# One fp32 matmul an image in place of three fp32r passes, with the identity added by VectorE

## The reference

```python
q, k, v = Wq x, Wk x, Wv x              # per image, 8 heads of 16 channels
k = softmax(k, axis=-2)                 # over the 16 channels of a head
context = einsum('bhdn,bhen->bhde', k, v)
out = einsum('bhdn,bhde->bhen', q, context)
y = einsum('oc,bchw->bohw', Wo, out) + x
mean, var = mean(y, axis=(0, 2, 3)), var(y, axis=(0, 2, 3))
result = (y - mean) * rsqrt(var + 1e-5) * gamma + beta
```

## Time and profile before

| | us |
|---|---|
| median of 3 runs | 53.73 |
| the runs | 52.9, 53.73, 54.81 |
| span of the profiled execution | 51.0 |
| TensorE busy | 37.5 |
| VectorE busy | 34.3 |
| ScalarE busy | 27.2 |
| GpSimd busy | 18.6 |

### The profile page before, as it was taken

One profiled execution on the slowest core, in us unless ns is written; L12 is line 12 of the kernel. 1 busy time (PEld: TensorE's weight loads), 2 busy tenths in 40 slices (PEclk: granted clock), 3 DMA queues, 4 the chain that ended last, 5 costly groups with the idle time before them and its releaser, 6 DMA issues.

```text
span 51.0 us, 1103 instructions
## 1 busy us (share of the span) xinstructions
PE 37.5 (74%) x377; PEld 32.5 (64%) x377; DVE 34.3 (67%) x90; ACT 27.2 (53%) x61; POOL 18.6 (37%) x28
## 2 busy tenths in 40 slices
PE   3999997892789799999999999999999700000000
PEld 3999996681877498888888979797969600000000
DVE  0028699923999986994996799763764989991000
ACT  3633918509799991494386179827246926500000
POOL 5820075974994989843016008180000000000000
PEclk9999999999999999999999999999999999995555
DMA  0499999700000000000000000000000000599993
GB/s 0 121 217 360 242 295 366 241 11 0 0 0 13 0 0 0 0 6 0 0 13 6 0 0 0 0 0 13 0 0 0 0 0 0 170 338 337 343 343 113
DMA packets 4741, 4.52 MB, mean 89 GB/s; under 512 B 384, under 2 KB 4736, under 8 KB 4736
## 3 DMA queue, kind: packets, MB, share of 16 engines
q1 hardware_dynamic: 4736, 4.46, 27.7%
HBM read 2.36 MB, written 2.10 MB: 87 GB/s over the span
## 4 chain that ended last, share of the span: by engine, by line
PE 47%; DVE 16%; DMA 14%; SPq 6%; issue 3%; ACT 2%; DVEq 1%; ACTq 0%
DMA x_sb<-x_dram 14%; PE banks L505 10%; PE banks L432 9%; PE banks L472 9%; PE banks L457 8%; PE banks L489 7%; DVE y_sb L413 6%; SPq L218 4%; PE banks L486 3%; DVE stats L386 3%; DVE k_max L341 3%; DVE k_sum L354 1%; ACT x_hi L282 1%; SPq L222 1%; DVEq L64 1%
## 5 line engine op out<-in xcount | busy, mean ns | idle before, releaser
L269 POOL TENSOR_TENSOR probs<-probs,k_inv 128x256 f32<-128x256 f32 (+1 forms) x11 | 8.9, 823 | 9.2 <-DVE k_inv L360 9.2
L261 POOL TENSOR_TENSOR x_lo<-x_sb,x_hi 128x512 fp32r<-128x512 f32 (+1 forms) x7 | 7.9, 1129 | 5.5 <-ACT x_hi L282 5.5
L432 PE MATMUL banks<-wkv_hi,x_hi 128*128 128x256 f32 x32 | 7.2, 309 | 1.4 <-ACT v_sb L293 1.4
L282 ACT ACTIVATE x_hi<-x_sb 128x256 fp32r<-128x256 f32 (+1 forms) x11 | 5.4, 512 | 5.3 <-DMA x_sb<-x_dram 5.2
L341 DVE TENSOR_REDUCE k_max<-banks 128x16 f32<-128x256 f32 (+1 forms) x11 | 5.7, 529 | 1.8 <-PE banks L432 1.7
L354 DVE TENSOR_REDUCE k_sum<-probs 128x16 f32<-128x256 f32 (+1 forms) x11 | 5.6, 531 | 1.8 <-ACT probs L287 1.8
L303 ACT ACTIVATE a_hi<-banks 128x256 fp32r<-128x256 f32 (+1 forms) x9 | 3.3, 362 | 6.6 <-PE banks L489 6.6
L432 PE MATMUL banks<-wkv_hi,x_lo 128*128 128x256 f32 x32 | 6.5, 284 | 0.3 <-POOL x_lo L261 0.3
L432 PE MATMUL banks<-wkv_lo,x_hi 128*128 128x256 f32 x32 | 6.5, 287 | 0.0
L432 PEld LDWEIGHTS banks<-wkv_hi,x_hi 128*128 128x128 f32 x32 | 5.0, 196 | 2.2 <-ACT x_hi L282 1.5
L472 PE MATMUL banks<-w_sb,ct_sb 64*64 64x128 f32 x64 | 5.2, 281 | 0.5 <-DVE ct_sb L368 0.5
(11 more groups left out here) (42 smaller groups left out, 57.7 us busy)
## 6 DMA issues: line engine op xcount, KB each, us to landing
x_sb<-x_dram SPq DMA_DIRECT2D x1, 1024.0 KB, 7.1
out_dram<-y_sb SPq DMA_DIRECT2D x2, 512.0 KB, 3.5
x_sb<-x_dram SPq DMA_DIRECT2D x3, 256.0 KB, 3.2
out_dram<-y_sb SPq DMA_DIRECT2D x3, 256.0 KB, 3.5
x_sb<-x_dram SPq DMA_DIRECT2D x2, 128.0 KB, 2.2
w_sb<-w_dram SPq DMA_DIRECT2D x2, 128.0 KB, 3.0
out_dram<-y_sb SPq DMA_DIRECT2D x2, 128.0 KB, 2.0
gamma_beta<-affine_dram SPq DMA_DIRECT2D x1, 1.0 KB, 6.8
```

What stands on the lines that cost most here:

```text
L261: nc.gpsimd.tensor_tensor(x_lo[:, p, px], x_sb[:, p, px], x_hi[:, p, px].bitcast(F32), ALU.subtract).then_inc(x_lo_ready, hi - lo)
L269: nc.gpsimd.tensor_tensor(heads, heads, inv.to_broadcast([128, (hi - lo) * CH * HEADS, D]), ALU.mult).then_inc(probs_ready, hi - lo)
L282: nc.scalar.activation(x_hi[:, p, px], x_sb[:, p, px], ACT.Copy).then_inc(x_hi_ready, hi - lo)
L432: last = nc.tensor.matmul(kv_ps(p)[:, g, :], xs[:, p, g * 128:(g + 1) * 128], ws[:, :], start=start and g == CH * image, stop=stop, skip_g ...
```

## The change

`a_hi` and `a_lo` are replaced by one fp32 tile `a_sb`. `times_wq` leaves the identity matmul out and writes A alone. VectorE's `add_identity` reads A from PSUM, adds the identity, which is now an fp32 tile, and writes `a_sb`; it stands where `split_a_lo` stood and waits for `a_ready` of TensorE. ScalarE's `split_a_hi` goes. `apply` runs one fp32 matmul an image, `a_sb` on `x_sb`. `times_wq` now has both of its waits, for `a_plus_one` and `u_copied`, ahead of its only matmul.

```diff
-        identity = sb("identity", [C, 2, C], BF16)
+        identity = sb("identity", [C, 2, C])
-        a_hi = sb("a_hi", [C, PAIRS, 2 * C], F32R)
-        a_lo = sb("a_lo", [C, PAIRS, 2 * C], F32R)
+        a_sb = sb("a_sb", [C, PAIRS, 2 * C])
...
-            def split_a_hi(p, lo, hi):
-                act.wait_ge(a_ready, 2 * p + hi)
-                nc.scalar.activation(a_hi[:, p, lo * C:hi * C], a_ps(p, lo, hi), ACT.Copy
-                                     ).then_inc(a_hi_ready, hi - lo)
...
-                      (split_a_hi, 3, CONTEXT), (copy_y, 4, CONTEXT, 0, IN_PSUM), (copy_u, 2, CONTEXT))
+                      (copy_y, 4, CONTEXT, 0, IN_PSUM), (copy_u, 2, CONTEXT))
...
-            def split_a_lo(p, lo, hi):
-                dve.wait_ge(a_hi_ready, 2 * p + hi)
-                nc.vector.tensor_tensor(a_lo[:, p, lo * C:hi * C], a_ps(p, lo, hi),
-                                        a_hi[:, p, lo * C:hi * C].bitcast(F32),
-                                        ALU.subtract).then_inc(a_lo_ready, hi - lo)
+            def add_identity(p, lo, hi):
+                dve.wait_ge(a_ready, 2 * p + hi)
+                nc.vector.tensor_tensor(a_sb[:, p, lo * C:hi * C], a_ps(p, lo, hi),
+                                        identity[:, lo:hi, :].rearrange("c b o -> c (b o)"),
+                                        ALU.add).then_inc(a_plus_one, hi - lo)
...
             def times_wq(p, lo, hi):
                 if p == 0:
-                    pe.wait_ge(consts_ready, 2)
                     pe.wait_ge(v_ready, 2 * (EXTRA + 1))
                 else:
-                    pe.wait_ge(a_lo_ready, 2 * p)
+                    pe.wait_ge(a_plus_one, 2 * p)
...
-                nc.tensor.matmul(a_ps(p, lo, hi), identity[:, 0, :], identity[:, lo:hi, :].rearrange("c b o -> c (b o)"),
-                                 start=True, stop=False)
                 pe.wait_ge(u_copied, 2 * p + hi)
-                nc.tensor.matmul(a_ps(p, lo, hi), wq, u_sb[:, p, lo * C:hi * C], start=False, stop=True
+                nc.tensor.matmul(a_ps(p, lo, hi), wq, u_sb[:, p, lo * C:hi * C], start=True, stop=True
                                  ).then_inc(a_ready, hi - lo)
...
             def apply(p, lo, hi):
-                pe.wait_ge(a_hi_ready, 2 * p + hi)
+                pe.wait_ge(a_plus_one, 2 * p + hi)
...
-                pass_over(a_hi, x_hi, True, False)
-                pass_over(a_hi, x_lo, False, False)
-                pe.wait_ge(a_lo_ready, 2 * p + hi)
-                last = pass_over(a_lo, x_hi, False, True)
+                for image in range(lo, hi):
+                    last = nc.tensor.matmul(y_ps(p, image, image + 1), a_sb[:, p, image * C:(image + 1) * C],
+                                            x_sb[:, p, image * N:(image + 1) * N],
+                                            start=image == lo, stop=True, skip_group_check=True)
                 last.then_inc(y_ready, hi - lo)
```

More of the change, by code:

```diff
@@ L149, in attention_batchnorm @@
         a_ready = sem("a_ready")
-        a_hi_ready = sem("a_hi_ready")
-        a_lo_ready = sem("a_lo_ready")
+        a_plus_one = sem("a_plus_one")
         y_ready = sem("y_ready")
@@ L390, in _ @@
                       (mask_context, 3, CONTEXT), (shift_keys, 0, SOFTMAX, 0, 2),
-                      (shift_keys, 0, SOFTMAX, 3, PAIRS), (sum_heads, 1, SOFTMAX), (split_a_lo, 4, CONTEXT),
+                      (shift_keys, 0, SOFTMAX, 3, PAIRS), (sum_heads, 1, SOFTMAX), (add_identity, 4, CONTEXT),
                       (invert_sums, 1, SOFTMAX), (shift_keys, 0, SOFTMAX, 2, 3), (count_y, 5, CONTEXT))
```

## The result

The changed kernel took 54.53 us, the median of 4 runs (54.31 to 54.64), against 53.31 for the kernel before over its 4 runs on that chip. The ratio is 1.027, with a 95% interval of 1.017 to 1.036: slower, while the interval leaves open whether by more or by less than 2%. Ratios and intervals in this document are taken from the faster runs of each kernel alone, so they are not the quotients of the medians (here 1.023). The forecast was 54.5, with 0.79 us of added work. The added work in the trace is 0.98 us, as follows.

What follows compares the result with a forecast made beforehand. TensorE was taken to bound the kernel from 17 to 40 us. Full slots 0.39, short slots 0.36 and the last pair 0.04 gave 0.79 us on 53.73: 54.5 us, 1.5% slower, 8-in-10 range 53.4 to 55.3.

Steps and rivals of the forecast that it cites:

- What bounds: From 17 to 40 us TensorE's stream sets the end; work taken from ScalarE or VectorE moves nothing.
- apply, 0.15 a pair: In `apply`, two fp32 matmuls at 0.86 us replace six fp32r ones at 0.71, adding 0.15 us a pair.
- The identity, worth 0.02 in a full slot: In `times_wq`, the identity streams while the next weights load anyway; dropping it gains 0.02 us a full slot, not 0.21.
- The first two rivals: Wq's load hides under `context`: -0.1 us, 53.7, chance 0.12; chain's 0.21 per identity is right: -0.4, 53.3, chance 0.06.
- One sign: Behind `context`: forecast wrong if L489's first stream started with its load; expected its record some 0.1 longer than the second.
- the two rules that were weighed: Behind `context`: tiling-mode change drains TensorE, identity worth 0.02 a slot; or loads are pulled ahead of matmuls, worth 0.13.
- Short slots, 0.12 each: In three slots without `project`, `apply` adds 0.15 us and the identity's going gains 0.03, between 0.00 and 0.06.
- The last pair, 0.04: At pair 6, `apply` adds 0.15 us and dropping the identity between the two images gains 0.11: sum 0.04.
- The third rival: Two waits ahead of `times_wq`'s one matmul open an issue gap, 0.10 to 0.11 in six slots: 55.2 us, chance 0.17.
- The cover of VectorE and ScalarE: VectorE's add replacing `split_a_lo` and ScalarE losing `split_a_hi` are worth nothing, being covered by TensorE's own stream.
- The sum: Three full slots 0.39, three short ones 0.36, the last pair 0.04: 0.79 us added to the median 53.73.
- Slower by over 2%: Whole kernel above 54.80 us: chance 0.33, from nearly all the two-waits case, a third of the forecast, and a small one.

Runs made afterwards that it cites:

- the other order: Kernel of before and changed kernel, each with TensorE running project, apply, times_wq, context, times_wo: 56.20 and 57.61 us against 53.14.

## Why the prediction was right, point by point

The direction and the mechanism held; the size was taken a fifth too small. That the time of 54.53 stands so near the forecast of 54.5 is luck: the forecast started from a median of 53.73 where the kernel of before came out at 53.31, and it added 0.79 where the medians differ by 1.22, and the two misses of 0.42 and 0.43 cancel.

- *What bounds.* Right. TensorE is busy for the whole of the full slots after the change too, and for 2.73 of 2.75 in a short one, and work taken from ScalarE moved nothing.
- *apply, 0.15 a pair.* Right: 0.86 for four records in every slot, against 0.71, and 0.88 against 0.73 in the last. The form of L489 was a good row for it.
- *The identity, worth 0.02 in a full slot.* Right, and the choice that mattered. The slots grew by 0.14, 0.12 and 0.15, or 0.41 in place of the forecast 0.39. Leaving it out of before alone showed it (0.06 over the three full slots), and in the other order, where the load can hide, the identity costs its own 0.12. The first two rivals, whose chances were 0.12 and 0.06, fall with this. One sign was put badly in the prediction: it would be wrong if L489's first stream started with the load. The record of that matmul does start with its load (both at 25.20), but a record's start doesn't show the stream's; its greater length of 0.10, which the prediction named too, is what shows the bare load. Of the two rules that were weighed, the trace sides with the drain at a change of tiling mode (TensorEngine Tiling (Array Packing) of the Trainium skill, section Key Properties): the load of Wq comes 0.62 behind the context's first load with and without the identity ahead of it.
- *Short slots, 0.12 each.* The step that was mis-sized. I took 0.03 for the identity's going between bounds of 0.00 and 0.06; it was 0.00, since the load waits for `copy_u`. The slots grew by 0.15, 0.17 and 0.15, 0.47 in place of 0.36. That `copy_u` stands behind `copy_y` was no limit: it starts 0.11 behind `times_wo` with `copy_y` ahead of it or not.
- *The last pair, 0.04.* It was 0.10. Between the first image's load of Wq and the first load of `apply` 0.11 was gained, as forecast (38.25 to 38.80 in the earlier trace rows, 40.14 to 40.58 now). But the first load now comes 0.11 behind the end of its copy (39.75 + 0.28 to 40.14), where L489's came 0.05 behind it with an identity matmul ahead (37.92 + 0.28 to 38.25). It is 0.11 in all the profiles of kernels in the old order without the identity matmul, and 0.05 in all those with it. The third rival, two waits ahead of one matmul, can have this much truth and no more: 0.06, once, where the rival had 0.10 in each of six slots. I can't say whether this is the second wait or TensorE having stood still; no run separates them, though in the short slots the second wait cost nothing.
- *The cover of VectorE and ScalarE.* Right. The add takes 418 ns, and the three counts are still back to back, 1.37 us.
- *The sum.* 0.79 forecast, 0.98 in the trace, 0.91 between the medians of the changed kernel's ten runs and of 40 of before. The other 0.24 of the measured 1.22 lie outside the stretch, where the runs of one kernel spread by 2 us; no experiment ties them to the landings of those runs. Slower by over 2% had a chance of 0.33 (its three parts, with a third of 0.57 as 0.19, come to 0.36). By the trace the change costs 0.98 on 53.7, 1.8%, and the ratio's interval holds 2%.

## What to carry to other kernels

The chain's price of an instruction is not what the kernel gains without it. Look at what the next instruction does beneath it: here a small matmul, the first behind a change of tile shape, hid the next weight load of 0.11 us, and so cost 0.02 in a full slot where the chain said 0.21. When an instruction is taken away on a bound engine, ask which load, drain or signal will be bare in its place, and read the bare price from a row where the trace already shows it. And where runs spread by a transfer at the start, compare a stretch that starts behind it: here it repeats to 0.01 us while the times move by 2 us.

## What the runs showed of the hardware

- A transfer of 1 MB with others ahead of it landed between 6.5 and 8.3 us after issue, over thirteen profiled executions of kernels that issue the same transfers.
- A late landing can cost twice: TensorE idle for about 1.9 us, and then a good three microseconds at the lower clock level, 0.79 us more. In another execution, with a pause of 1.2 us in the same place, the clock stayed, and so it did after a pause of 1.96 us in another kernel.
- At each change of tile shape the next weight load comes some 0.07 us before the modelled end of the matmul ahead, with one, two or more waits in front of it, unless a signal comes later (0.01 before that end for Wq in the short slots). The first load behind the change is bare if it has 128 columns of fp32 or fp32r: the matmul record that starts with it is 0.10 us longer (0.48 against 0.38, 0.38 against 0.28). The bf16 identity's record behind a change is 0.28, as long as the one where no change stands ahead.
